# A transformer block with routed experts: attention's small tiled matmuls become block-diagonal ones, fed by DMA

## The reference

```python
h = layer_norm(x, ln1_w, ln1_b)
q, k, v = (einsum('btc,hcs->bhts', h, W) for W in (Wq, Wk, Wv))
wei = softmax(where(causal, einsum('bhts,bhus->bhtu', q, k) * C ** -0.5, -1e30))
attn = einsum('bhtu,bhus->bhts', wei, v).transpose(0, 2, 1, 3).reshape(B, T, C)
x = x + attn @ Wo + bo
nx = layer_norm(x, ln2_w, ln2_b)
noisy = nx @ Wr + br + noise * softplus(nx @ Wn + bn)
router_out = softmax over the two largest of noisy, per token
skip = sigmoid(nx @ Wsk + bsk) > 0.5
expert_out = sum over e of router_out[e] * (relu(nx @ W1[e] + b1[e]) @ W2[e] + b2[e])
return x if skip else x + expert_out
```

## Time and profile before

| what | us |
|---|---|
| median of 3 runs | 1028.79 (1027.72 to 1032.57) |
| the profiled execution | 1030.05 |
| its span | 1028.3 |
| PE busy | 643.3 |
| DVE busy | 557.5 |
| ACT busy | 505.0 |
| POOL busy | 422.2 |

### The profile page before, as it was taken

One profiled execution on the slowest core, in us unless ns is written; L12 is line 12 of the kernel. 1 busy time (PEld: TensorE's weight loads), 2 busy tenths in 40 slices (PEclk: granted clock), 3 DMA queues, 4 the chain that ended last, 5 costly groups with the idle time before them and its releaser, 6 DMA issues.

```text
span 1028.3 us, 31440 instructions
## 1 busy us (share of the span) xinstructions
PE 643.3 (63%) x11084; PEld 476.9 (46%) x11084; DVE 557.5 (54%) x2095; ACT 505.0 (49%) x1081; POOL 422.2 (41%) x488
## 2 busy tenths in 40 slices
PE   4775676567656765675577556517999999972000
PEld 2463454345434543454345444415777777762000
DVE  4653444344534453444354435444777777761998
ACT  5664355445544544455345533416887788860000
POOL 6314334433443344334433443660665565553000
PEclk9787678767876786787678766657999999995555
DMA  8911211211112112111215600027667767741998
GB/s 231 329 55 49 73 41 45 67 51 41 45 57 58 40 45 74 42 41 45 68 49 142 131 16 13 20 105 261 213 231 235 221 219 242 230 132 52 324 338 281
DMA packets 131020, 127.32 MB, mean 124 GB/s; under 512 B 21154, under 2 KB 109315, under 8 KB 130976
## 3 DMA queue, kind: packets, MB, share of 16 engines
q1 hardware_dynamic: 101792, 102.58, 32.6%
q0 software_dynamic: 12288, 15.77, 4.8%
q10 hardware_dynamic: 16896, 8.39, 2.7%
HBM read 73.86 MB, written 62.78 MB: 133 GB/s over the span
## 4 chain that ended last, share of the span: by engine, by line
PE 57%; issue 27%; DVE 7%; DMA 2%; ACT 2%; DVEq 2%; SPq 1%; another core or an unknown queue 1%; POOL 1%; POOLq 0%; ACTq 0%
PE ps L580 8%; PE ps L555 6%; PE ps L590 5%; PE ps L593 4%; PE ps L602 4%; PE ps L627 3%; PE ps L646 3%; PE ps L691 3%; PE ps L693 3%; PE ps L659 3%; PE ps L692 3%; PE ps L703 3%; PE ps L704 2%; PE ps L705 2%; DVE z L1133 2%
## 5 line engine op out<-in xcount | busy, mean ns | idle before, releaser
L1209 POOL DMA_INDIRECT expert_rows<-pay,rows_of x256 | 252.6, 987 | 372.1 <-DVE rows_of L1023 299.4
L580 PE MATMUL ps<-kT,qT 32*32 32x32 f32 x4096 | 91.9, 228 | 210.2 <-issue 208.3
L1226 POOL DMA_INDIRECT expert_results<-z,words x128 | 130.8, 1022 | 121.4 <-DVE z L1100 77.7
L580 PEld LDWEIGHTS ps<-kT,qT 32*32 32x32 f32 x4096 | 65.7, 123 | 235.5 <-issue 232.1
L968 DVE TENSOR_REDUCE smax<-ps 128x16 f32<-128x512 f32 x32 | 22.1, 691 | 208.6 <-PE ps L580 208.6
L778 ACT ACTIVATE qT<-ps 128x512 f32<-128x512 f32 x32 | 19.0, 594 | 208.4 <-PE ps L590 208.4
L1114 DVE TENSOR_TENSOR hlo<-h,hhi 128x512 fp32r<-128x512 f32 x128 | 88.8, 694 | 58.4 <-ACT hhi L860 40.3
L734 ACT ACTIVATE z<-xres,shift,rstd 128x128 f32 (+1 forms) x256 | 105.0, 482 | 30.6 <-DVE shift L962 24.9
L858 ACT ACTIVATE h<-ps,w1x 128x512 f32<-128x512 f32 x128 | 88.7, 693 | 46.6 <-PE ps L693 36.4
L860 ACT ACTIVATE hhi<-ps,w1x 128x512 fp32r<-128x512 f32 x128 | 88.2, 689 | 0.0
L590 PE MATMUL ps<-hT,wq 128*128 128x512 f32 x64 | 64.4, 1108 | 9.7 <-ACT hT L757 9.7
(11 more groups left out here) (154 smaller groups left out, 1365.3 us busy)
## 6 DMA issues: line engine op xcount, KB each, us to landing
w1x<-split_weights SPq DMA_DIRECT2D x33, 514.0 KB
w2x<-split_weights SPq DMA_DIRECT2D x33, 512.5 KB
expert_results<-zeros SPq DMA_DIRECT2D x32, 512.0 KB
pay<-expert_rows SPq DMA_DIRECT2D x33, 264.0 KB
xres<-in_r_x SPq DMA_DIRECT2D x32, 256.0 KB, 5.7
hhi<-expert_results SPq DMA_DIRECT2D x16, 512.0 KB, 5.6
hlo<-expert_results SPq DMA_DIRECT2D x16, 512.0 KB, 5.6
out<-z ACTq DMA_DIRECT2D x32, 256.0 KB, 5.9
```

Source lines behind the costliest of these rows:

```text
L580: m = nc.tensor.matmul(ps[b * T:(b + 1) * T, h, j * T:(j + 1) * T], qT[h * HS:(h + 1) * HS, at], kT[h * HS:(h + 1) * HS, at], start=False, ...
L1209: g.indirect_dma_start(rows, bass.IndirectOffsetOnAxis(ap=rows_of[:, odd, k * J + j:k * J + j + 1], axis=0), pay[:, odd, k, j, :], None, b ...
L1226: g.indirect_dma_start(results, bass.IndirectOffsetOnAxis(ap=words[:, slot, j:j + 1], axis=0), yrow[slot][:, j, :], None, bounds_check=K * ...
```

## The change

The scores of one sequence for all four heads become one matmul. For that the keys stand in a block-diagonal tile k_bd: row quarter h holds the keys of head h in column block h, and zeros elsewhere. The weighted values of one head for the four sequences of a tile become one matmul in the same way, against p_bd, the transposed probabilities in a block diagonal over sequences. So there are 16 matmuls of a 128x32 stationary tile and 128 moving columns for the scores, into one PSUM bank, and 16 for the weighted values. One mask matmul of 512 columns takes the place of four.

k_bd and p_bd lie in hhi and hlo. POOL sets them to zero once; in each step SP fills the diagonal with four DMAs of 64 KB for the keys (after kT was copied) and four for the probabilities (after pT). SP's loop becomes the same pipeline of steps: probabilities of t - 1, x of t + 3, zeros of group t, keys of t + 1. Zeros of groups 0 to 4 come after the pipeline. The loads of raw weights 2 to 7 and all stores of the cut ones move from SP to ACT, at the end of ACT's steps.

In PE's order the value projection comes right after the weighted values and ahead of the rank counts. PSUM banks are dealt out anew (scores 0, weighted values 1, transposes 2, output projection 3), and some waits between users of a bank go.

```diff
+        k_bd, p_bd = hhi[:].bitcast(F32), hlo[:].bitcast(F32)
...
+            def spread_k(n):
+                apart(sp, (s_k_copied, n + 1),
+                          (s_s_made, n))
+                for h in range(H):
+                    part = slice(h * HS, (h + 1) * HS)
+                    sp.dma_start(k_bd[part, h], kT[part]).then_inc(s_k_bd, 16)
+
+            def spread_p(n, par):
+                apart(sp, (s_pT_made, n + 1),
+                          (s_o_made, n))
+                for b in range(NB):
+                    part = slice(b * T, (b + 1) * T)
+                    sp.dma_start(p_bd[part, b], pT[part, par].rearrange("p j h t -> p (j h t)")).then_inc(s_p_bd, 16)
+
+            def step(t, par):
+                odd = 1 - par
+                n = t - 1
+                if live(n):
+                    spread_p(n, odd)
+                n = t + 3
+                if live(n) and not (isinstance(n, int) and n < EARLY):
+                    load_x(n, odd)
+                n = t
+                if live(n) and not (isinstance(n, int) and n < LATE):
+                    zero_results(n)
+                n = t + 1
+                if live(n):
+                    spread_k(n)
...
-            with sp.Fori(8, NG - 1, 2) as n:
-                load_x(n, 0)
-                zero_results(n)
-                load_x(n + 1, 1)
-                zero_results(n + 1)
-            for n in range(8):
+            sp.wait_ge(s_bd_zeroed, 2)
+            pipeline(nc.sync, step)
+            for n in range(LATE):
                 zero_results(n)
...
-                    apart(pe, (s_k_copied, n + 1),
-                              (s_oT_made, n - 1),
+                    apart(pe, (s_k_bd, n * BD + BD),
                               (s_s_less, n))
...
-                    for h in range(H):
-                        nc.tensor.matmul(ps[:, h, 0:P], ident16[:], mask16[:].rearrange("p j t -> p (j t)"),
-                                         start=True, stop=False)
+                    nc.tensor.matmul(ps[:, S_BANK, :].rearrange("p (a u) -> p a u", u=T), ident16[:],
+                                     mask16[:].unsqueeze(1).to_broadcast([P, J * H, T]), start=True, stop=False)
                     for j in range(J):
                         for b in range(NB):
-                            for h in range(H):
-                                at = slice(j * P + b * T, j * P + (b + 1) * T)
-                                m = nc.tensor.matmul(ps[b * T:(b + 1) * T, h, j * T:(j + 1) * T],
-                                                     qT[h * HS:(h + 1) * HS, at], kT[h * HS:(h + 1) * HS, at],
-                                                     start=False, stop=(j == J - 1),
-                                                     tile_position=(h * HS, b * T))
+                            at = slice(j * P + b * T, j * P + (b + 1) * T)
+                            m = nc.tensor.matmul(ps[b * T:(b + 1) * T, S_BANK, j * P:(j + 1) * P], qT[:, at],
+                                                 k_bd[:, :, at], start=False, stop=(j == J - 1),
+                                                 tile_position=(0, b * T))
...
-                    apart(pe, (s_pT_made, n + 1),
-                              (s_s_less, upto(n + 2)))
+                    apart(pe, (s_p_bd, n * BD + BD),
+                              (s_v_copied, n + 1))
                     for j in range(J):
                         for h in range(H):
-                            for b in range(NB):
-                                m = nc.tensor.matmul(ps[h * HS:(h + 1) * HS, b, P + j * T:P + (j + 1) * T],
-                                                     v_sb[b * T:(b + 1) * T, odd, j, h * HS:(h + 1) * HS],
-                                                     pT[b * T:(b + 1) * T, odd, h, j, :], start=True, stop=True,
-                                                     tile_position=(b * T, h * HS))
+                            m = nc.tensor.matmul(ps[h * HS:(h + 1) * HS, O_BANK, j * P:(j + 1) * P],
+                                                 v_sb[:, odd, j, h * HS:(h + 1) * HS],
+                                                 p_bd[:, :, (j * H + h) * T:(j * H + h + 1) * T],
+                                                 start=True, stop=True, tile_position=(0, h * HS))
                     m.then_inc(s_o_made, 1)
...
+                for e in splits(t - 1):
+                    store_cut(e)
+                    if e + 4 < E:
+                        load_raw(e + 4)
                 for e in splits(t):
...
+            load_raw(2)
+            load_raw(3)
             nc.scalar.preload_act_table_set("natural_log_exp_and_others")
...
+            g.memset(k_bd, 0.0).then_inc(s_bd_zeroed, 1)
+            g.memset(p_bd, 0.0).then_inc(s_bd_zeroed, 1)
```

## The result

The changed kernel takes 997.52 us (median of 4 runs, 994.33 to 1003.43), the kernel before 1028.32 us (4 runs, 1027.72 to 1032.57): a ratio of 0.970, 95% interval 0.966 to 0.973. That is 31 us or 3% less. The profiled execution took 997.75 us, with a span of 995.2. The median lies 26 us above the forecast of 971, inside the stated range of 915 to 1045, but outside the 950 to 990 that the forecast's own rival (a) had for itself.

What follows compares the result with a forecast made beforehand. Bound: each 20.45 us routing step, PE's stall during POOL's scatters plus the way from its release to the next scatter. 1030.05 - 66 (27 steps at 18.0) + 8 (start) = 972, or 971 as a median; range 915 to 1045.

Steps and rivals of the forecast that it cites:

- rival (a): Routing steps: the forecast itself, stall stays, queries and keys slip into it; 971 us, 950 to 990; chance 0.48.
- A stall that stays, with its release at S + 11.7: Routing step: POOL's scatters hold PE; S is the first scatter's start, PE's release comes 11.7 us later.
- What has finished isn't told until R: Routing step: ACT and DVE learn of PE's finished work only at PE's release, R, about 1 us after POOL's last operation.
- Part 1: PE's instruction count: 314 records a step fall to 119; 43 pass by the release, so queries and keys fit the stall.
- Part 2: New block-diagonal matmuls: 32 records of 128 columns take 1.3 us, with 3.9 or 5.8 us as the other end.
- rival (b): New matmuls: the four 32-column strips take turns, 21.3 us a step, 1060 us; chance 0.12.
- Part 3: Order after PE's release: next first scatter 6.3 us later, so 18.0 us a step, 2.45 less; 27 steps give -66 us.
- Part 4: Eight new DMAs a step: keys land 7.1 us after PE's release, scores can start at 7.9; 0.8 us of cover.
- Part 5: Start, with ACT's added stores and loads and the key DMAs: +8 us, bounds -5 and +23; tail and zeroing 0.
- (c): Stall: keys come late or fewer than 43 records pass, queries and keys run after it; 1041 us, half 1006; chance 0.18.
- (d): Stall belongs to the number of instructions and goes away with 119 records: 13 us a step, 837 us; chance 0.07.
- (e): Stall: more passes in it than counted, weighted values too; 16.1 us a step, 921 us; chance 0.15.

Runs made afterwards that it cites:

- a_hot_first: Changed kernel with PE's rank counts ahead of the value projection and DVE's routing chain ahead of the maxima: 1034.33 us, ratio 1.002 to the kernel before.

## Why the prediction was right, step by step

- **A stall that stays, with its release at S + 11.7.** Measured S + 11.62 to S + 11.87 in six traces, and S + 13.3 to 13.5 in their fifteenth steps, whose scatters are late. Right, as the size and as the tie to POOL's work. The prediction called it a property of POOL's scatter work; the runs at 781 us show the same scatters without it. So it needs more than they, and in that the step was too sure.
- **What has finished isn't told until R.** The maxima start 0.2 us after R in the changed kernel, and `a_hot_first` shows the price when that for hT and the scores fall in the stall: 2 us a step.
- **Part 1, 119 records a step, 43 of which pass.** Measured 3316 in 28 steps, 118.4, and 49 from S before the stall plus four in it. Queries and keys slipped in wholly in about every other step, as at 312.44, where the scores begin with the second scatter, and those steps take 18.6 to 18.7 us. In the others PE is behind: at 293.38 it is still in the router logits at the second scatter, the stall begins in the scores, the last keys start only at R, and such steps take 0.5 us more in the mean (19.06 for that one, 19.64 at 404.68, 20.53 at 365.46, right behind the step of 15.74). "With little to spare" was right for half of the steps and too hopeful for the other half.
- **Part 2, 32 records of the new form in 1.3 us.** Measured 1.08 us at full clock, 0.034 us a record; rival (b), 3.9 us, is out. By the Trainium skill (TensorEngine Tiling (Array Packing), Key Properties), tiles operate independently, which gave 1.0 us: the trace agrees. But after R the last 27 took 1.93 us at half clock.
- **Part 3, R to the next S in 6.3 us.** Measured 6.9 us, and here lies the first missed term. hot_any started at R + 3.22 and ended at R + 3.42 (R + 3.2 was taken), and from the ranks' end to S' it was 1.9 us as taken. But PE got to the ranks only at R + 3.87, since 1.93 us of weighted values and 2.08 us of value projection both ran at half clock (granted clock 0.50 from 324.20 to 328.10), where 3.2 us at most was allowed; and the ranks took 1.1 us, not 0.8. The prediction kept the weighted values at the 1.3 us of their old place, though its own row of the stretch behind R had a granted clock of 0.50, and its change moved them there. PE, not hot_any, came last. The period was thus 18.65 us instead of 18.0: 0.65 by 28 steps is 18 us of the 26 missed. The late-key steps are in this mean, and so is the one of 15.74 us.
- **Part 4, eight DMAs a step hidden.** In the steady steps PE has no wait for them; the mask waits for keys three times in the whole span (18.5 us), all in steps 0 to 2. SP issued keys at 327.06 (R + 2.8; R + 2.6 was taken). That the keys are hidden held, but the sum R + 7.1 is only bounded: the mask came at R + 9.4 instead of R + 7.9, so PE's own lateness gave 1.5 us more cover than was planned. The rule of the Trainium skill that such transfers serialize (DMA: Bandwidth & Descriptors, Rules for kernel authors) gave, with that page's fit for one transfer, an estimate of R + 11.3 for the keys; the mask of the next step starts at 333.57, R + 9.4, with no wait for them, so here the trace speaks against the full sum.
- **Part 5, the start at +8 us.** Measured +15.3, the second missed term: 7 us. The step had the right cause, ACT's issues with everything else queued behind, and mis-sized it: 0.5 us an issue from a quiet row, where the 24 in ACT's steps took 0.9 us each, 22.4 us. Its other rows had this, for the four stores on SP took 5.73 us. The keys were given 4 steps by up to 2 us; their waits are 18.5 us, but only some 3 us of the first two stand on the way of the queries. A DMA was priced by a quiet moment, both its issue and its landing, in a stretch that is not quiet. The tail and the zeroing: 0.8 us against 0.
- The rivals: (c) came true in part, for the keys of about half of the steps, not by late key DMAs but by fewer records than were needed; it priced such a step at 2.6 us more than the forecast's, and it was 0.5. (d), that the stall vanishes with fewer instructions, did not happen in the pair. (e), the weighted values in the stall too, came in the fifteenth step alone, at 15.74 us against the 16.1 of its sum.

The two terms, 18 and 7 us, are 25 of the 26 by which the time missed the forecast. The mechanism was right and the gain came at little over half of its size, 31 us of the 57 forecast. The number stayed inside the range because that was made to hold rivals (c) and (e) as well.

## What to carry to other kernels

When one engine is held for a fixed time in each step, fewer instructions pay only through what then fits in front of and inside the hold; ask which work it will catch, and at which clock the rest follows. Moving the step's trigger earlier can cost the whole gain, since it moves the hold onto other work and other signals (`a_hot_first`). And transfers added to the start of a kernel are not priced by their issue and landing elsewhere: look at the busy share of the DMA engines there (0.89 here), and at what stands behind the issues on the engine that makes them (0.9 us each here).

## What was not expected of the hardware

The same kernel before took 1028 to 1030 us in two sets of runs and 781 to 782 us in two others, on different chips. In the traces at 1028 and of the changed kernel at 997, PE is held from S + 3 or 4 to S + 11.6 or a little later in each ordinary step; in the eight at 781 to 954 us there is no such hold, though the scatters take the same 0.97 us each; where nothing else is late there, POOL alone sets a step of 11.3 us. So the verdict on the change itself depends on whether the hold is there: a ratio of 0.970 with it, and without it no gain that these runs could show (its nearest kin gave 1.001 and 1.014). That it is the chip that decides is the plain reading, but no chip was used in two of the three groups, so something else that differed between the groups isn't excluded. By what way POOL's scatters reach TensorE stays open.
